# One expert-mixture layer on one core: h turned by transfers and VectorE, a lag of three tiles, and another front

## The reference

```python
base   = einsum('btd,od->bto', x, W)                       # 512 x 512
logits = einsum('btd,ed->bte', x, Wr) + 5.0 * one_hot(language_id)
topw, topi = top_k(logits, 2);  weights = softmax(topw)
gates  = sum(one_hot(topi) * weights)                      # b, t, 8
h      = einsum('btd,erd->bter', x, A)                     # b, t, 8, 16
cond   = base + 2.0 * einsum('bter,bte,eor->bto', h, gates, B)
out    = x + einsum('bsi,io->bso', cond, sign) * softplus(scale)
```

## Time and profile before

| what | value |
|---|---|
| median of 3 runs | 164.6 us (164.39 to 165.2) |
| the profiled execution's own time | 164.64 us |
| its span, first to last instruction | 162.8 us |
| PE busy | 158.3 us (97%) |
| DVE, ACT, POOL busy | 97.6, 66.0, 52.1 us |
| DMA, 16 engines | 36.5% + 2.0% of the span |

### The profile page before, as it was taken

How to read it: one execution, slowest core, us unless ns; L and a number is a source line. 1 busy time by engine, 2 the same in 40 slices (tenths; PEclk the granted TensorE clock), 3 DMA queues, 4 the chain that set the end, 5 groups by cost and what they waited for, 6 DMA issues and landing times.

```text
span 162.8 us, 3711 instructions
## 1 busy us (share of the span) xinstructions
PE 158.3 (97%) x1070; PEld 153.8 (94%) x1070; DVE 97.6 (60%) x416; ACT 66.0 (41%) x177; POOL 52.1 (32%) x50
## 2 busy tenths in 40 slices
PE   7999998999999999999999999999999999999993
PEld 5788897999999999999999999999999999999992
DVE  5689997555556665554554555556665555455741
ACT  3654722434344333344444343344333344443440
POOL 2994453332222233333333322222333333333000
PEclk9999999999999999999999999999999999999998
DMA  4996323424333333334333333333333333111113
GB/s 170 380 146 136 90 82 101 131 70 146 105 122 114 124 119 115 124 129 129 129 129 127 104 101 117 112 121 123 113 123 120 128 129 129 64 64 64 68 66 129
DMA packets 29431, 19.51 MB, mean 120 GB/s; under 512 B 7248, under 2 KB 24432, under 8 KB 29424
## 3 DMA queue, kind: packets, MB, share of 16 engines
q1 hardware_dynamic: 28496, 18.23, 36.5%
q10 hardware_dynamic: 928, 1.20, 2.0%
HBM read 11.03 MB, written 8.39 MB: 119 GB/s over the span
## 4 chain that ended last, share of the span: by engine, by line
PE 90%; DVE 7%; issue 1%; ACT 0%; DVEq 0%
PE pair L643 66%; PE pair L679 14%; PE p_b L577 2%; PE p_ht L686 2%; PE pair L589 2%; DVE m_full L470 2%; PE pair L596 2%; PE pair L603 2%; DVE xt L432 1%; DVE wide_lo L476 1%; DVE gate L547 1%; DVE b_lo L501 0%; DVE b_lo L487 0%; DVE wide_lo L483 0%; ACT y L395 0%
## 5 line engine op out<-in xcount | busy, mean ns | idle before, releaser
L300 POOL TENSOR_TENSOR xt_lo<-xt,xt_hi 128x512 fp32r<-128x512 f32 x32 | 41.6, 1299 | 91.5 <-ACT xt_hi L348 91.5
L643 PE MATMUL pair<-wide_hi,xt_hi 128*128 128x392 f32 (+1 forms) x248 | 60.8, 321 | 0.0
L643 PE MATMUL pair<-wide_hi,xt_lo 128*128 128x392 f32 (+1 forms) x248 | 58.3, 311 | 0.0
L643 PE MATMUL pair<-wide_lo,xt_hi 128*128 128x392 f32 (+1 forms) x248 | 58.3, 311 | 0.0
L643 PEld LDWEIGHTS pair<-wide_hi,xt_lo 128*128 128x128 f32 x248 | 38.6, 188 | 0.0
L643 PEld LDWEIGHTS pair<-wide_lo,xt_hi 128*128 128x128 f32 x248 | 38.5, 188 | 0.0
L643 PEld LDWEIGHTS pair<-wide_hi,xt_hi 128*128 128x128 f32 x248 | 38.3, 189 | 0.1
L394 ACT ACTIVATE y<-pair 128x256 f32<-128x256 f32 x31 | 11.9, 384 | 44.3 <-PE pair L679 44.3
L516 DVE TENSOR_TENSOR logits<-pair,bias 128x8 f32<-128x8 f32 x32 | 5.3, 165 | 35.7 <-PE pair L643 35.7
L432 DVE STREAM_TRANSPOSE xt<-x_in 128x512 f32<-128x512 f32 x32 | 22.7, 710 | 3.7 <-DVE top L524 3.2
L348 ACT ACTIVATE xt_hi<-xt 128x512 fp32r<-128x512 f32 x32 | 20.3, 633 | 2.8 <-DVE xt L432 2.8
(11 more groups left out here) (82 smaller groups left out, 142.0 us busy)
## 6 DMA issues: line engine op xcount, KB each, us to landing
x_in<-in_x SPq DMA_DIRECT2D x128, 64.0 KB, 1.9
out<-y SPq DMA_DIRECT2D x31, 256.0 KB, 2.1
sign_in<-in_L_ffn_sign ACTq DMA_DIRECT2D x4, 256.0 KB, 5.1
w_in<-in_L_cond_W SPq DMA_DIRECT2D x4, 256.0 KB, 4.9
a_in<-in_L_cond_A SPq DMA_DIRECT2D x4, 64.0 KB, 5.1
b_in<-in_L_cond_B SPq DMA_DIRECT2D x4, 64.0 KB, 4.2
out<-y SPq DMA_DIRECT2D x1, 128.0 KB, 1.7
out<-y ACTq DMA_DIRECT2D x1, 128.0 KB, 1.8
```

Of the source, the lines that this page charges most:

```text
L300: nc.gpsimd.tensor_tensor(xt_lo[n][:, :, :].rearrange("p j (g b) -> p g j b", g=NQ), xt[n][:, :, :, :], xt_hi[n][:, :, :].bitcast(FP32).re ...
L643: last = nc.tensor.matmul(pair[n][bank][:, at0:at0 + hi - lo], l[:, k, :], w[:, k, lo:hi], start=(opens and k == 0 and l is xt_hi[n] and w ...
```

## The change

1. **h without TensorE.** For tiles 0 to 28 the transposition by matmul goes. SP waits for `h_gated` of a tile and issues four transfers from SBUF to SBUF (`move_h`), each of 128 rows of 32 numbers, 128 bytes, into 32 partitions of `h_moved`; VectorE then turns 128 x 128 numbers in blocks (`turn_h` of VectorE) into `ht` in SBUF, ScalarE makes `ht_hi` from it and VectorE `ht_lo`, both with an output stride of four numbers. Tiles 29, 30 and 31 (`late`) go through TensorE as before, into PSUM banks of pairs that are free then.
2. **Lag and ring.** The lag is 3 instead of 2, all rings have four slots instead of three; `p_ht` and `p_b2` go, and b2 is summed in `pair[3][0]`.
3. **Transfers of x.** Tiles 4 and 5 are loaded by SP at the start; from tile 6 on ScalarE's queue issues the four transfers, in step s for tile s+5, after its exponential and before the copies of y.
4. **Front.** scale and language ids are loaded in 4 rows and spread by a VectorE transposition, in place of 128 packets of 4 bytes; scale follows W's second quarter on SP, the last quarter of sign goes from ScalarE's queue to SP's, after W. The first chunk of W and of sign is cut and multiplied in halves. Warm-up matmuls read a constant, so they don't wait for a memset, and are 19 instead of 18. The softplus chain lies between the low parts of W. b's high part comes before A's on ScalarE, its low part before A's on VectorE. x of tile 3 is turned ahead of b2's low part, both in step 1.
5. **End.** `finish` does `wide` for bank 0 of tiles 30 and 31 with `lora` of 27 and 28, then bank 1 with `lora` of 29 and 30, then `lora` of 31.

The core of the diff:

```diff
+    RING = 4
-        LAG = 2
+        LAG = 3
+        LATE = TILES - 3
@@ SP
             for j in range(OC):
                 sp_eng.dma_start(w_in[:, j, :], w_load[:, j, :]).then_inc(w_loaded[j], 16)
+                if j == 1:
+                    sp_eng.wait_ge(rows_zeroed, 2)
+                    sp_eng.dma_start(scale_rows[0:P:Q, :], scale.partition_broadcast(NQ)).then_inc(scale_loaded, 16)
+            sp_eng.dma_start(sign_in[:, OC - 1, :], sign_load[:, OC - 1, :]).then_inc(sign_loaded[OC - 1], 16)
...
+            for t in range(RING, RING + 2):
+                sp_eng.wait_ge(xt_made, t - RING + 1)
+                load(1, t - RING, t)
+            def move_h(q, r, d):
+                n = slot(r, d)
+                sp_eng.wait_ge(h_gated_made, RING * q + r + d + 1)
+                for i in range(NQ):
+                    sp_eng.dma_start(h_moved[n][Q * i:Q * i + Q, :, :], h_gated[n][:, Q * i:Q * i + Q])\
+                        .then_inc(h_arrived[n], 16)
             def turnover(q, r, s):
-                if s is None or s + S3 < TILES:
-                    sp_eng.wait_ge(xt_made, S3 * q + r + 1)
-                    load(q, r, S3 * q + r + S3)
+                if s is None or 0 <= s - LEAD - 1 < LATE:
+                    move_h(q, r, -LEAD - 1)
                 if s is None or s >= LAG + LEAD:
                     store(q, r, -LAG - LEAD)
@@ ScalarE
+            act.wait_ge(b_loaded, 16 * OC)
+            nc.scalar.activation(b_hi[:, :, :, :], b_in[:, :, :, :], ACT.Copy).then_inc(b_hi_made, 1)
             act.wait_ge(head_turned, 1)
...
+            def load(q, r, d):
+                n = slot(r, d)
+                act.wait_ge(xt_made, RING * q + r + d + 1 - RING)
+                for i in range(NQ):
+                    act.dma_start(x_in[n][Q * i:Q * i + Q, :, :], x_load[i, :, RING * q + r + d, :, :])\
+                        .then_inc(x_loaded[n], 16)
+            def high_h(done, late):
+                if late is None:
+                    act.wait_ge(ht_made, done - LAG + 1)
+                    nc.scalar.activation(ht_hi[:, :].rearrange("p (b g) -> p g b", g=NQ), ht[:, :, :], ACT.Copy)\
+                        .then_inc(ht_hi_made, 1)
+                else:
+                    act.wait_ge(ht_turned, late - LATE + 1)
+                    act.wait_ge(y_summed, late)
+                    nc.scalar.activation(ht_hi[:, :], p_ht[late][:, 0:P], ACT.Copy).then_inc(ht_hi_made, 1)
             def step(q, r, s):
+                if s is None or 0 <= s - LAG < LATE:
+                    high_h(RING * q + r, None)
                 if has(s, -1):
...
+                if s != 0 and has(s, 1 + RING):
+                    load(q, r, 1 + RING)
+                if s in (TILES - 1, TILES, TILES + 1):
+                    high_h(s, s - 2)
@@ VectorE
-            def low_h(done):
-                dve.wait_ge(ht_hi_made, done - LAG + 1)
-                nc.vector.tensor_tensor(ht_lo[:, :], p_ht[:, 0:P], ht_hi[:, :].bitcast(FP32), ALU.subtract)\
+            def low_h(done, late):
+                dve.wait_ge(ht_hi_made, done - LAG + 1 if late is None else late + 1)
+                if late is None:
+                    nc.vector.tensor_tensor(ht_lo[:, :].rearrange("p (b g) -> p g b", g=NQ), ht[:, :, :],
+                                            ht_hi[:, :].bitcast(FP32).rearrange("p (b g) -> p g b", g=NQ),
+                                            ALU.subtract).then_inc(ht_lo_made, 1)
+            def turn_h(q, r, s):
+                n = slot(r, -LAG)
+                dve.wait_ge(h_arrived[n], 16 * NQ * (turn(q, r, -LAG) + 1))
+                nc.vector.transpose(ht[:, :, :].rearrange("p g b -> p (g b)"),
+                                    h_moved[n][:, :, :].rearrange("p g c -> p (g c)")).then_inc(ht_made, 1)
             def step(q, r, s):
...
+                if s is None or 0 <= s - LAG < LATE:
+                    turn_h(q, r, s)
+                if s == TILES:
+                    low_h(done, TILES - 3)
                 if has(s, -1):
                     nc.vector.max(top[:, :], logits[:, :]).then_inc(top_made, 1)
+                if s is None or 0 <= s - LAG < LATE:
+                    low_h(done, None)
-                if s == 0:
-                    turn_x(q, r, LEAD, first=True)
-                    low_b2()
+                if has(s, LEAD) and s != 1:
+                    turn_x(q, r, LEAD, first=(s is not None and s + LEAD < RING))
...
+                if s == 1:
+                    turn_x(q, r, LEAD, first=True)
+                    low_b2()
@@ TensorE
-                nc.tensor.matmul(p_b2[:, 0:2 * P], warm[:, 0:P], warm[:, :], start=True, stop=True)
+                nc.tensor.matmul(p_b2[:, 0:2 * P], nc.const_aps.tensor(1.0, [P, P], BF16),
+                                 nc.const_aps.tensor(1.0, [P, 2 * P], BF16), start=True, stop=True)
...
-                if has(s, -1):
-                    turn_h(done)
             def finish(s):
...
+                wide(before, second, (BANKS[1],))
+                wide(r, first, (BANKS[1],), opens=True)
                 pe.wait_ge(ht_lo_made, s)
                 lora(before, (0, 1)).then_inc(y_summed, 1)
+                turn_h(s)
+                wide(r, second, (BANKS[1],))
                 pe.wait_ge(ht_lo_made, s + 1)
+                lora(r, (0,)).then_inc(last_summed, 1)
+                lora(r, (1,)).then_inc(y_summed, 1)
```

More of the change, by code:

```diff
@@ L98, in adaln_ffn_kernel @@
         ln_one = sb("ln_one", [P, 1])
-        x_in = [sb(f"x_in{n}", [P, NQ, P]) for n in range(S3)]
-        xt = [sb(f"xt{n}", [P, NQ, KC, Q]) for n in range(S3)]
-        xt_hi = [sb(f"xt_hi{n}", [P, KC, P], FP32R) for n in range(S3)]
-        xt_lo = [sb(f"xt_lo{n}", [P, KC, P], FP32R) for n in range(S3)]
+        x_in = [sb(f"x_in{n}", [P, NQ, P]) for n in range(RING)]
+        xt = [sb(f"xt{n}", [P, NQ, KC, Q]) for n in range(RING)]
+        xt_hi = [sb(f"xt_hi{n}", [P, KC, P], FP32R) for n in range(RING)]
+        xt_lo = [sb(f"xt_lo{n}", [P, KC, P], FP32R) for n in range(RING)]
         logits = sb("logits", [P, E])
@@ L164, in adaln_ffn_kernel @@
         b2_lo_made = sem("b2_lo_made")
-        x_loaded = [sem(f"x_loaded{n}") for n in range(S3)]
-        y_stored = [sem(f"y_stored{n}") for n in range(S3)]
+        x_loaded = [sem(f"x_loaded{n}") for n in range(RING)]
+        y_stored = [sem(f"y_stored{n}") for n in range(RING)]
         xt_made = sem("xt_made")
@@ L182, in adaln_ffn_kernel @@
         h_gated_made = sem("h_gated_made")
+        h_arrived = [sem(f"h_arrived{n}") for n in range(RING)]
+        ht_made = sem("ht_made")
         ht_turned = sem("ht_turned")
@@ L327, in _ @@
         def _(act):
-            for j in range(OC):
+            for j in range(OC - 1):
                 act.dma_start(sign_in[:, j, :], sign_load[:, j, :]).then_inc(sign_loaded[j], 16)
@@ L604, in high_low @@
                                      skip_group_check=True)
-            high_high(0)
+            pe.wait_ge(first_half_made, 1)
+            pe.wait_ge(first_sign_made, 1)
+            for k in range(KC):
+                if k == 2:
+                    pe.wait_ge(w_hi_made, 1)
+                nc.tensor.matmul(p_m[k][:, 0:HALF], w_cols(w_hi, 0, k), sign_hi[:, 0, 0:HALF], start=True, stop=False,
+                                 skip_group_check=True)
+            pe.wait_ge(early_sign_hi_made, 1)
+            for k in range(KC):
+                nc.tensor.matmul(p_m[k][:, HALF:D], w_cols(w_hi, 0, k), sign_hi[:, 0, HALF:D], start=False, stop=False,
+                                 skip_group_check=True)
             low_high(0)
@@ L681, in lora, with turn_h @@
                 return last
-            def turn_h(done):
-                pe.wait_ge(h_gated_made, done)
-                nc.tensor.transpose(p_ht[:, 0:P], h_gated[:, :], ident[:, :]).then_inc(ht_turned, 1)
+            def turn_h(tile):
+                pe.wait_ge(h_gated_made, tile + 1)
+                nc.tensor.transpose(p_ht[tile][:, 0:P], h_gated[tile % RING][:, :], ident[:, :]).then_inc(ht_turned, 1)
             def step(q, r, s):
-                done = S3 * q + r
+                done = RING * q + r
                 if s == 0:
@@ L705, in step @@
                     wide(r, range(KC // 2, KC), BANKS, signals=True)
[L706 to L707 removed]
             def finish(s):
[L711 removed]
+                before, r = (s - 1) % RING, s % RING
                 first, second = range(KC // 2), range(KC // 2, KC)
                 pe.wait_ge(xt_lo_made, s)
[L715 to L717 removed]
@@ L718, in finish @@
-                lora(slot(before, -LAG), (0, 1)).then_inc(y_summed, 1)
-                wide(before, second, (BANKS[0],)).then_inc(head_ready, 1)
-                turn_h(s - 1)
-                pe.wait_ge(xt_lo_made, s + 1)
-                pe.wait_ge(y_copied, s - S3 + 1)
-                wide(r, first, (BANKS[0],), opens=True)
-                pe.wait_ge(ht_lo_made, s - LAG + 1)
```

(21 more changed lines are left out.)

206 lines of the change are left out of this document (109 added, 97 removed).

## The result

The kernel after takes 163.91 us (median of 20 runs, 163.26 to 164.4), the kernel before, on the same chip, 164.7 (20 runs, 164.22 to 165.92): ratio 0.9934 [0.9916, 0.9952]. The profiled execution took 163.53 us, with a span of 161.3 against the 159.3 of the sum; 2.23 us lie outside the span (before: 1.84). The spans of its 20 runs go from 161.1 to 162.2, with a median of 161.7, so the profile shows one of the shorter ones.

What follows compares the result with a forecast made beforehand. PE, busy for 97% of the span, was taken as the bound. Span 162.8 - 3.05 (transpositions) - 0.89 (wait before step 2) + 0.24 (end) + 0.2 (stalls) = 159.3; with 1.84 around it 161.1 us, range 160.3 to 163.2.

Steps and rivals of the forecast that it cites:

- the sum: The prediction's addition of gains and costs over the whole kernel, giving a span of 159.3 us.
- the wait before step 2: Between steps 1 and 2 PE waits for gated h of tile 0; the longer lag was to save 0.89 us.
- h landing late: Rival: moved h lands late in the loop, slower than before from a landing of 4.2 us; chance 6%.
- rival 4: Transposition hidden behind weight loads, so only the wait before step 2 goes: 163.9 to 164.5 us; chance 2%.
- the price of the transposition: In the loop, 29 transpositions leave PE at 0.105 us each: 3.05 us less.
- Rival 2: ScalarE's queue issues x late, delaying y and `ht_lo`; PE waits in each of 26 steps: 162.4 to 163.7 us; chance 15%.
- The 0.44 before PE: Loop margin: `ht_lo`, if held behind `xt_lo`, is ready at 1.35 us and PE wants it at 1.79; cost 0.
- Step 3: First `lora` in the new order, needing h of tile 0: margin 0.3 us, cost 0, bounds 0 and 0.5.
- the 0.2 allowance: 0.2 us added for stalls of a few tenths in steps 3 and 4, where four margins meet.
- The front: Start of the kernel, up to the low parts of M: cost 0, bounds -0.3 and +0.6 us.
- The end: Before the last `lora`, six matmuls instead of nine cover the last transposition: PE idles 0.24 us, bounds 0.1 and 0.6.
- rival 1: The forecast case with its bounds in the front, at step 3 and at the end: 160.4 to 162.0 us; chance 62%.

Runs made afterwards that it cites:

- one_turn: The kernel before with TensorE turning h of tile 0 only and using it for every tile: 162.55 us, ratio 0.9868 to the kernel before.
- load_halves: The kernel after with two of ScalarE's four x transfers issued behind `xt_hi` instead of ahead of y: 162.99 us, ratio 0.9889 to the kernel before.

## Why the prediction was wrong, point by point

- **Direction and mechanism** were right: PE bounds, the transposition and the wait before step 2 leave the chain, SP and the landing keep up. Of the rivals, h landing late did not occur in the loop (1.8 us; the sum had 1.9). The measured 163.91 is a number of rival 4, which gave 163.9 to 164.5 for a transposition that costs nothing; but it cost 0.08 of the 0.11, so this is a coincidence and not the mechanism. By the Trainium skill ("DMA: Bandwidth & Descriptors", section "Why small descriptors are slow (HBM only)") SBUF to SBUF is exempt from the penalty of small descriptors; the trace agrees for 128-byte pieces, by the 1.8 us.
- **The failed step is the price of the transposition.** "Each costs PE 0.11 us in the chain ... I take 0.105": it was 0.08, shown by one_turn. The piece in the chain and the difference 4.38 - 4.27 both assumed that `wide` and `lora` would pass into each other for 4.275. 29 x 0.105 = 3.05 should have been 29 x 0.08 = 2.3. This is the largest single term, 0.7 of the 2.0 us of span; alone it moves the forecast only to 161.8. That 163.91 lies above the stated range took the terms below as well, none of which went the other way by much.
- **Rival 2 was real.** "It fits with 0.13 to spare" held in only 8 of 24 steps; the four issues took 2.0 us in the mean where the sum had 1.82. The 0.44 before PE covered this except in steps 8, 12 and 20. The working of the rival was right in each link (y, `xt_hi`, `xt_lo`, `ht_lo`); it had 0.05 to 0.1 in each of 26 steps, and it was 0.06, 0.06 and 0.30 in three, 0.42 us in all. It was treated as a case beside the forecast, where a part of it should have been in the sum. load_halves shows it.
- **Two sizes that ate the margin.** The stride "could be twice as long": it was 1.5 times on `ht_hi` and 1.4 on `ht_lo`, and the sum left both at their old length, so of the 0.44 us before PE some 0.2 were gone. Issuing a move costs 0.6, above the upper end (1.9 us for four; 2.5 measured).
- **Step 3.** "Margin 0.3; cost taken 0, bounds 0 and 0.5": PE's idle time is 0.16, and in the sum's terms it is 0.33, or 0.43 with the longer distance behind the wait. `second` at 1.10 us, the moves at 0.6, a last landing of 2.94 us where the sum had 1.9, and the stride made it; it lay in the bounds, and the 0.2 allowance covered a part.
- **The front** was costed without the new small operations on VectorE. `scale_spread` met GpSimd's low part of sign and took 1.27 us. Though the prediction told of the `gate` row, it applied it only to `ht_lo`. The Trainium skill ("SBUF — State Buffer", section "SBUF: two separate sides") has this exclusion for VectorE operations with two SBUF inputs and for its two-port modes. The trace agrees in that an operation of 128 x 32 numbers took 1.27 us beside GpSimd's; it has one tensor and one number per partition as inputs, and no run shows which of the two cases it was. +0.3 lay within the bounds of -0.3 and +0.6.
- **The end.** The last wait was right to 0.02, in part by luck: 0.14 of later start where 0.24 was forecast, and 0.11 for the slower start of `lora` behind a wait, which the sum didn't have. Missed were `lora` of tile 29, 0.14, and the wait of bank 0 of tile 31 for the first half of y of tile 27, 0.27: an added wait for which nobody asked who is queued behind it.
- **Outside the span.** "With the 1.84 around the span" was carried over, and it is 0.4 short: 2.2 us lie outside the span in the runs of the kernel after and in those of every edit of it, 1.8 in those of the kernel before and of one_turn. So it comes with the change; which part of it brings it stays open. The other 0.4, by which the median lies above the profiled execution, is the spread of the spans.
- **The range.** The upper end of rival 1, 162.0, is less than its own bounds give: 0.6 + 0.5 + 0.36 above 161.1 is 162.6, or 162.4 without the allowance.

## What to carry to other kernels

A short instruction between long ones is worth the difference of two measured periods, one of them without it; its own piece of the chain is an upper end. Before a transfer is put into an engine's own queue, add up what stands behind it in that engine's order: here moving two of four issues behind the last urgent activation took away all stalls of the loop, while giving them to the other queue made the kernel 2.5% slower than the one before, and some 3% slower than the one it was an edit of. A VectorE operation whose operands all lie in SBUF and that can meet a GpSimd one is to be costed at the length of that one, however small it is: here this held for `scale_spread`, `second`, `gate` and, in part, `ht_lo`. And a wait costs TensorE more than its idle time: here some 0.1 us more, each time.

## What the hardware showed that was not expected

- Issuing a transfer from SBUF to SBUF with pieces of 128 bytes takes SP's queue 0.6 us in the median (four mostly in 2.49 to 2.59, at most 3.45), one of x from HBM 0.37 in the median on ScalarE's queue and 0.32 on SP's in the kernel before, though the first lands sooner (1.8 against 2.2 us).
- After a wait the second matmul of a `lora` starts 0.21 to 0.22 us after the first, without one 0.12.
- An access of 128 x 128 float32 with a step of four numbers takes 433 ns instead of 311 on ScalarE, 0.40 instead of 0.29 on VectorE's subtraction and 414 instead of 312 in its turning (there on the written side); on ScalarE and in the subtraction a read with this step costs about as much as a write (445 ns, 0.39 us).
- VectorE operations of 8 and 32 columns take 1.10 and 1.27 us beside GpSimd's (0.29 for the same `second` in step 7).
- The first matmuls of 256 columns come every 0.213 us and later ones every 0.117, with the change at 3.9 to 6.5 us from one execution to another, while the granted clock reads 1.00.
